# Delta stage of a four-part kernel: the second pair's scaled keys ahead of its scans, three more products of q ahead of their transposes

## What is computed

```python
q = x @ Wq + bq
kr = x @ Wk + bk
k = kr / jnp.maximum(jnp.linalg.norm(kr, axis=-1, keepdims=True), 1e-12)
v = x @ Wv + bv
alpha = jax.nn.sigmoid(x @ Wa + ba)
beta = jax.nn.sigmoid(x @ Wb + bb)
gate = jax.nn.sigmoid(x @ Wg + bg)
def step(S, inp):
    Sk = jnp.einsum('bij,bj->bi', S, k_t)
    S_new = a * (S - b * (Sk[:, :, None] * k_t[:, None, :])) + b * (v_t[:, :, None] * k_t[:, None, :])
    o = jnp.einsum('bi,bij->bj', q_t, S_new) * g_t
```

## Time and profile before

| what | us |
|---|---|
| median of 3 runs | 2375.0 |
| lowest and highest | 2374.38, 2377.75 |
| the profiled execution | 2378.28 |
| its span, first to last instruction | 2376.3 |

### The profile page before, as it was taken

How to read it: one execution, slowest core, us unless ns; L and a number is a source line. 1 busy time by engine, 2 the same in 40 slices (tenths; PEclk the granted TensorE clock), 3 DMA queues, 4 the chain that set the end, 5 groups by cost and what they waited for, 6 DMA issues and landing times.

```text
span 2376.3 us, 37595 instructions
## 1 busy us (share of the span) xinstructions
PE 2294.8 (97%) x12333; PEld 1927.7 (81%) x12333; DVE 1545.4 (65%) x2938; ACT 1193.1 (50%) x2353; POOL 783.1 (33%) x1329
## 2 busy tenths in 40 slices
PE   7999999999699999999999999999999999999997
PEld 5898888988578888888888888888888788888886
DVE  3566665666666675666767667666676766666666
ACT  3444444444443344343443434533443577777775
POOL 2555555555511211211112011121111135555555
PEclk8999999999899999999999999999999999999999
DMA  5122122232600300202002020020120333333322
GB/s 137 54 80 97 44 97 106 79 115 82 189 1 1 107 1 18 89 0 78 29 18 89 0 71 35 18 89 0 43 95 18 120 111 106 106 106 106 106 89 71
DMA packets 101736, 166.38 MB, mean 70 GB/s; under 512 B 19665, under 2 KB 22481, under 8 KB 101521
## 3 DMA queue, kind: packets, MB, share of 16 engines
q1 hardware_dynamic: 97328, 163.69, 20.4%
q10 hardware_dynamic: 4320, 1.71, 0.3%
HBM read 115.05 MB, written 50.33 MB: 70 GB/s over the span
## 4 chain that ended last, share of the span: by engine, by line
PE 69%; DVE 1%; POOL 1%; issue 0%; ACT 0%; POOLq 0%; DVEq 0%
PE quant_bank L1517 7%; PE quant_bank L1516 7%; PE quant_bank L1515 7%; PE quant_bank L1905 6%; PE quant_bank L1907 6%; PE quant_bank L1906 6%; PE quant_bank L1542 5%; PE quant_bank L1543 5%; PE quant_bank L1544 5%; PE quant_bank L1532 4%; PE quant_bank L1561 3%; PE quant_bank L1563 3%; PE quant_bank L1562 2%; PE quant_bank L1504 1%; PE quant_bank L1922 1%; PE quant_bank L1573 1%
## 5 line engine op out<-in xcount | busy, mean ns | idle before, releaser
L1356 POOL TENSOR_SCALAR quant_var<-quant_mv 128x1 f32<-128x1 f32 x256 | 56.0, 219 | 1008.6 <-DVE quant_mv L1431 1008.6
L1384 ACT ACTIVATE quant_g_hi<-quant_bank,kept_beta,kept_gamma 128x512 fp32r<-128x512 f32 x192 | 150.6, 785 | 395.6 <-PE quant_bank L1532 395.6
L1515 PE MATMUL quant_bank<-kept_W_hi,quant_h_hi 128*128 128x512 f32 x768 | 305.5, 398 | 0.0
L1516 PE MATMUL quant_bank<-kept_W_lo,quant_h_hi 128*128 128x512 f32 x768 | 303.5, 395 | 0.0
L1517 PE MATMUL quant_bank<-kept_W_hi,quant_h_lo 128*128 128x512 f32 x768 | 303.4, 395 | 0.0
L1429 DVE BATCH_NORM_STATS2 quant_stats<-quant_bank 128x6 f32<-128x512 f32 x192 | 134.0, 698 | 190.2 <-PE quant_bank L1517 190.1
L1870 DVE TENSOR_TENSOR mlp_g_lo<-quant_bank,mlp_g_hi 128x512 fp32r<-128x512 f32 x256 | 176.4, 689 | 105.3 <-ACT quant_bank L1807 105.2
L1806 ACT ACTIVATE mlp_g_hi<-quant_bank,mlp_b 128x512 fp32r<-128x512 f32 x256 | 177.3, 693 | 70.9 <-PE quant_bank L1907 63.6
L1542 PE MATMUL quant_bank<-quant_g_hi,kept_W_hi 128*128 128x512 f32 x512 | 205.2, 401 | 0.0
L1543 PE MATMUL quant_bank<-quant_g_hi,kept_W_lo 128*128 128x512 f32 x512 | 202.5, 396 | 0.0
L1544 PE MATMUL quant_bank<-quant_g_lo,kept_W_hi 128*128 128x512 f32 x512 | 202.4, 395 | 0.0
(11 more groups left out here) (280 smaller groups left out, 5901.7 us busy)
## 6 DMA issues: line engine op xcount, KB each, us to landing
delta_x_in<-L_attn_x_d SPq DMA_DIRECT2D x16, 1024.0 KB, 8.1
delta_x_res<-L_attn_x_d SPq DMA_DIRECT2D x16, 1024.0 KB, 5.6
x_d<-delta_z SPq DMA_DIRECT2D x64, 256.0 KB, 2.1
kept_x_in<-x_d SPq DMA_DIRECT2D x16, 1024.0 KB, 5.2
quant_y<-x_d SPq DMA_DIRECT2D x16, 1024.0 KB, 5.0
x_d<-quant_y SPq DMA_DIRECT2D x16, 1024.0 KB, 4.4
mlp_x_in<-x_d SPq DMA_DIRECT2D x16, 1024.0 KB, 10.4
mlp_x_res<-x_d SPq DMA_DIRECT2D x16, 1024.0 KB, 6.4
```

The costliest lines, as they stand in the source:

```text
L1384: nc.scalar.activation(g_hi[m][:, k, :], tr[k][:, :], ACT.Gelu, bias=beta[:, b, k:k + 1], scale=gamma[:, b, k:k + 1])
L1515: mm(out, x_hi, W_hi[2 * b][:, k, :], start=False, stop=False, skip_group_check=True)
L1516: mm(out, x_hi, W_lo[2 * b][:, k, :], start=False, stop=False, skip_group_check=True)
```

## The change

In the string ORDER three things move: kh.1 goes ahead of decay.1; q.6 q.7 q.8 go ahead of kT.1 (and A.1 and M.0); kk.1 goes behind q.9 q.10 q.11.

```diff
-            q.0 q.1 q.2 kk.0 MnT.0 decay.1 q.3 q.4 q.5 kh.1 kT.1 A.1 M.0 q.6 q.7 q.8 W0.0 kk.1 q.9 q.10 q.11 qout.0 MnT.1 g.0 g.1 g.2 M.1 g.3 g.4 g.5 W0.1
+            q.0 q.1 q.2 kk.0 MnT.0 kh.1 decay.1 q.3 q.4 q.5 q.6 q.7 q.8 kT.1 A.1 M.0 W0.0 q.9 q.10 q.11 kk.1 qout.0 MnT.1 g.0 g.1 g.2 M.1 g.3 g.4 g.5 W0.1
```

## The result

The changed kernel takes 2349.7 us (median of 4 runs, 2349.3 to 2351.2) against 2376.4 for the kernel before (4 runs). The ratio is 0.989 with a 95% interval of 0.9872 to 0.9907. The gain is 26.7 where 26.5 was forecast; the prediction was 2348.5, in a range of 2345.5 to 2356. The profiled execution went from a span of 2376.3 to 2349.2, 27.1 less.

What follows compares the result with a forecast made beforehand. TensorE, busy 97%, was bound by idle waits for VectorE's scaled keys. Units 1 to 13 gain 20.5, unit 0 1.3, unit 15 1.5, unit 14 3.5: 26.8, rounded to 26.5, so 2375.0 becomes 2348.5 us, range 2345.5 to 2356.

Steps and rivals of the forecast that it cites:

- The bound: Delta stage: TensorE's second-pair key transposes (L956) wait for VectorE's scaled keys (L751), 23.2 us over 16 units.
- kh.1's end: VectorE, steady unit: kh.1 ends 0.28 behind GpSimd's diag.1, at 327.93, going ahead of the ready ogT_lo.
- the rival in which GpSimd goes first: kh.1 also waits for ogT_lo; only the products gain, 0.70 per unit, 11.8 in all, time 2363; chance 0.08.
- kT.1 and M.1: TensorE, steady unit: kT.1 starts at 328.32, 0.88 earlier, M.1 2.27 behind it; 1.63 us gained per unit.
- No slack at MnT.1: MnT.1 releases M.1 at 330.59, exactly when TensorE has done kk.1 and g.0 to g.2; slack is nil.
- the charge of 0.05: Taken off the 1.63 gained per unit for MnT.1's nil slack, in units 1 to 13.
- Unit 14 and the clock: Unit 14 gains 3.5, of which 1.6 comes from no longer falling to the granted clock of 0.51.
- Slack of kk.1: kk.1 on TensorE has 0.23 left after the release of ScalarE's copy of kT.1.
- The tail: The two stages behind the delta stage are TensorE's own and begin earlier by as much, taking nothing back.
- The range: Forecast spans 2345.5 (nothing charged, 28) to 2351.5, chance 0.71; range goes on to 2356, into the wait-is-left rival.
- The rival of a lower clock: TensorE without pauses gets its lower clock; two such stretches per unit cost 24.7 more, time 2400; chance 0.03.

Runs made afterwards that it cites:

- two experiments on ogT_lo: GpSimd's ogT_lo moved behind part.2 in the kernel before (2371.3 us), and ahead of diag.1 in the changed kernel (2365.6 us).
- products alone: Kernel before with q.6 to q.8 ahead of kT.1 and kk.1 behind q.9 to q.11, kh.1 staying behind the scans: 2365.7 us.
- one product's move: Changed kernel with M.1 ahead of g.2 in place of behind it: 2353.6 us.
- keys alone: Kernel before with only kh.1 moved ahead of decay.1, TensorE keeping its order: 2356.5 us against 2377.5.
- low part later: Kernel before with GpSimd's ogT_lo behind part.2 in place of behind diag.1: 2371.3 us.
- low part ahead: Changed kernel with GpSimd's ogT_lo ahead of diag.1 in place of behind it: 2365.6 us.
- the three variants of it below 2354: Changed kernel with M.1 ahead of g.2 (2353.6 us); with kk.1 between q.10 and q.11 (2350.6); with last unit's LoRA roundings moved later (2343.3).

## Why the prediction was right

- *The bound.* The waits of L956 were the lost time, and nearly all of them went.
- *kh.1's end.* Forecast 0.28 behind diag.1, measured 0.27 to 0.29 behind it, with VectorE ahead of the ready ogT_lo in units 1 to 15. The two experiments on ogT_lo show the cause. What the rival in which GpSimd goes first would have given is nearest to the products alone, where kh.1 ends behind ogT_lo: 0.61 a unit, and 1.6 more in unit 14, which its sum of 11.8 had left out. The Trainium skill, "SBUF — State Buffer", section "SBUF: two separate sides", has the exclusion for a whole instruction, and the runs agree with it (0.27 to 0.29 behind the end of the GpSimd instruction, at rows of 0.51 to 1.45).
- *kT.1 and M.1.* Forecast 0.93 and 2.27 apart from q.5 and kT.1, measured 0.92 and 2.29 in unit 8 (2.28 in most).
- *No slack at MnT.1.* Right, and shown by one product's move. With the charge of 0.05 a unit was to gain 1.58, and 1.57 was measured. Hardly any of the 0.05 stands in front of M.1; 0.03 to 0.04 lies between its two transposes (0.14 and 0.15 apart, 0.11 before).
- *Unit 14 and the clock.* The kernel before had 2.03 of idle there and then a granted clock of 0.51. Four other runs had between 0.78 and 1.63 of idle in the same place (keys alone 0.80, products alone 1.33, low part later 1.63, low part ahead 0.78) and a granted clock of 1.00 there. Each gained 1.6 to 1.8 in that unit beyond its steady gain. The other five traces, in which kT.1 of that unit waits about 0.3 (the changed kernel twice and the three variants of it below 2354), show 1.00 there too. So one trace falls, at the longest wait, and nine do not; that the fall hangs on the wait is what they bear out, but there is only this one trace of the kernel before. Why 2.03 is enough and 1.63 not stays open, and I did not try to find the point. The wait of 0.16 that comes 6 us ahead of the 2.03 does not tell them apart, for the other four have it too (0.16 or 0.17).
- *Slack of kk.1.* I gave it 0.23 to spare. Taking 0.23 away left it just touched, by 0.06, so the figure was some 0.05 too large. It had no effect on the time.
- *The tail.* I took it as moving whole. It moved by 25.6 to 27.5 from place to place, as its short stretches at the lower clock fell at other moments. Two traces of the changed kernel alone show the same: they are 1.0 apart behind the last unit and 2.4 apart behind the tail. So the agreement unit by unit tests the prediction, and that the whole agrees to 0.2 is in part luck.
- *The range.* Its lower end does not follow from its words: 28 off 2375.0 is 2347, not 2345.5. The result lies above both.
- *The denser TensorE.* The rival of a lower clock did not come: 36.88 of 37 us of work at 1.00.

## What to carry to other kernels

In an order written by hand ask of each instruction in front of a wait whether the waiting side needs it; here two scans and a wait on GpSimd stood ahead of a short product that TensorE was waiting for. Two edits on the two sides of one wait are not additive: work out the distance that each leaves, and then which instruction comes late next, since the slack that an interleaved block of products gave one chain is taken from another. Where a VectorE instruction reads two inputs from SBUF, look at what GpSimd runs at the moment when the VectorE instruction starts, and place the long GpSimd instructions elsewhere.

## What the runs showed of the hardware

- A VectorE product with two SBUF inputs (128x256, 0.40 alone) ended 0.27 to 0.29 behind the end of the GpSimd instruction that ran when it started, at rows of 0.56, 0.81, 1.13 and 1.41. A GpSimd instruction ready behind that one let VectorE go first, and grew by 0.17 to 0.21 (1.26 to 1.47, 0.62 to 0.79).
- VectorE did not go first twice running. In unit 15 of the kernel before, kh.0 went ahead of the second add; VectorE's next instruction, which also reads two inputs from SBUF, then took 1.77 where it took 0.68 just before (at 580.32), and ended 0.55 behind the add's end at 583.70:

```profile
582.48 1.77 DVE L863 SCALAR_TENSOR_TENSOR delta_rows<-delta_rows,delta_scale 128x512 f32<-128x512 int32 x1
```

- VectorE's scans and products with one input in PSUM kept their durations beside GpSimd: decay.1 took 0.72 to 0.74 beside ogT_lo and alone, MnT.0 0.42 beside diag.1.
- A granted clock of 0.51 for some 3.5 us followed a wait of 2.03 in one trace, and none followed waits of 1.63 and less in the same place in nine.
